# A rewritten attention phase: scores on row halves of TensorE, three bank pairs, and steps moved between engines

## The chip, the cores and the metric

The kernel runs on one core of a Trainium2 chip. The metric is the device time of one execution in microseconds (us). Engines: PE (TensorE, matmuls), PEld (its weight loads), DVE (VectorE), ACT (ScalarE), POOL (GpSimd), SP (SyncE, which here only issues DMAs). Lines L1 to L1629 are those of the kernel before.

## The reference, cut to what matters

Eight batches of 512 tokens with 256 channels go through one transformer layer in float32: a pre-norm causal attention with 16 heads of 16 channels and rotary positions, and then a mixture of 8 experts, 2 for each token.

```python
q = (x @ Wq.T + bq).reshape(b, t, h, dh).transpose(0, 2, 1, 3)      # k, v likewise; x is layer-normed
q = _apply_rope(q, cos, sin); k = _apply_rope(k, cos, sin)
scores = jnp.einsum('bhqd,bhkd->bhqk', q, k) / jnp.sqrt(dh)
scores = jnp.where(causal, scores, -jnp.inf)
out = jnp.einsum('bhqk,bhkd->bhqd', jax.nn.softmax(scores, -1), v)
x = x + out @ Wo.T + bo
logits = layernorm(x) @ router_w + router_b                         # top 2 of 8 experts, capacity 153
o = silu((e @ w_c_fc + b_c_fc) * (e @ w_gate + b_gate)) @ w_c_proj + b_c_proj
x = x + sum_k prob_k * o[expert_k, position_k]
```

## The kernel before

The program has two phases. The attention phase (`attention_phase`, L104) handles the 8 batches, the expert phase (`expert_phase`, L1081) the 8 experts; the second is the same in both kernels apart from a few semaphore counts.

**Groups and slots.** The 16 heads of a batch are 4 groups of 4 heads (g = 0 to 3). Each group takes 8 slots (u = 0 to 7), so a batch is 32 slots, and every engine has a `body_slot(b, g, u)` that issues its share in slot order. Batches 2 to 6 run in a hardware loop on each engine, the others are written out.

**Two passes over the scores.** In slot u, `pass1` (L392) makes the scores of query block i = u // 2 against all keys up to it, for the two heads of pair u % 2, and DVE takes their row maximum (`reduce_max`, L794). The maxima of a group are turned (piece M), negated on ACT (L584), and sent by DMA as one more row of the query stack (`send_max`, L333). Two groups later `pass2` (L412) makes the scores again, transposed (key block j = u // 2), now with the maximum subtracted inside the product, and ACT takes the exponential (L569, L577) into `probs`. `pv` (L437) multiplies them with V in 32-column tiles of the array, one for each of the 4 heads; being plain float32, each of its matmuls appears as two in the trace.

**The stacks.** q and k are split into a large and a small part so that three products give float32 accuracy. They go to DRAM (`store_hilo`, L315) and come back stacked (`load_stack`, L320): 64 rows, (large, small) of q against (large, large) and (small, small) of k, a row of ones and the row of the maximum. A score matmul so contracts over 65 or 66 rows of the 128. Ahead of it a bf16 matmul of a mask with the identity writes the causal mask into the bank.

**Banks.** Pass 1 uses PSUM banks 0 to 3 as two pairs, pass 2 bank 4 or 5 for one head (or two heads of 256 columns), the V product bank 6, everything else bank 7.

**Pieces.** Everything else that PE does for a batch is a piece with a slot of its own in `PIECES` (L235): X turns the normalised input of the next batch, Q is one of its four q and k projections, V its value projection, M and A turn maxima and attention output, T and O are the output projection of the batch before, H, L, R, F the router of the one before that. The rotary step is a shuffle, a multiplication by sin and a sum on DVE (L811 to L817) and a multiplication by cos on POOL (L935); the split is on POOL (L947, L950). The layer norm statistics and both normalisations (L695) are on DVE, the reciprocal square root on POOL (L898). POOL also scatters the tokens to their expert slots (L964). Some steps of the last batches are placed into the first expert by `LATE_SLOTS` (L1069).

**What sets the order.** Each engine runs its own list in program order; a wait on a semaphore holds back all that is behind it on that engine. A DMA issued by SP waits for its own condition and holds back the DMAs behind it.

## Time and profile before

| | us |
|---|---|
| median of 3 runs | 1383.12 (1378.21 to 1386.19) |
| the profiled execution | 1391.76, of it 1389.9 from the first to the last instruction |
| attention, from the first maximum to the last | 40.7 to about 593 |
| expert phase in its steady part and tail | about 691 to 1389.9 |

| engine | busy us | share |
|---|---|---|
| PE | 1238.5 | 89% |
| PEld | 1023.6 | 74% |
| DVE | 729.6 | 52% |
| POOL | 697.0 | 50% |
| ACT | 496.3 | 36% |

The granted TensorE clock is 0.943 of full speed on average. A busy PE in this profile holds the drain of each matmul too, so 89% is not 89% of what the array could do. The shares are averages over two phases with different limits, so the stages are read one by one.

### The profile page before, as it was taken

How to read it: one execution, taken by the hardware profiler on the slowest of the kernel's cores; microseconds unless marked ns; L12 is line 12 of the kernel's file. 1: busy time of each engine (PE TensorE's matmuls, PEld its weight loads, DVE VectorE, ACT ScalarE, POOL GpSimd, SP SyncE). 2: the span in 40 equal slices, each digit the busy share in tenths (PEclk: the TensorE clock that was granted, in tenths of full speed). 3: DMA queues.
4: the chain of work that ended last, by engine and by line, in shares of the span. 5: the costliest groups of instructions: out<-in, count | busy, mean ns of one | idle time of the engine just before them, and what ended most of it. 6: DMA issues, size and time to landing. Idle time of an engine off the chain costs nothing.

```text
span 1389.9 us, 25801 instructions
## 1 busy us (share of the span) xinstructions
PE 1238.5 (89%) x8360; PEld 1023.6 (74%) x8360; DVE 729.6 (52%) x1512; ACT 496.3 (36%) x988; POOL 697.0 (50%) x984
## 2 busy tenths in 40 slices
PE   3699999999898989988899999999999999997830
PEld 3465656566565656548899999999999999997730
DVE  5777776858676767556333343343333433333336
ACT  2145444535353535454223332333233332332100
POOL 4334243343425251267755665576656764634445
PEclk9699999999999999999999999999999999998865
DMA  5766545444434453432312211131122112102247
GB/s 138 216 208 193 177 115 144 109 132 103 138 93 139 100 149 93 137 124 60 96 62 91 70 62 62 64 98 54 66 78 87 54 58 70 64 28 72 69 131 249
DMA packets 82333, 147.86 MB, mean 106 GB/s; under 512 B 9263, under 2 KB 59832, under 8 KB 78142
## 3 DMA queue, kind: packets, MB, share of 16 engines
q1 hardware_dynamic: 64576, 111.37, 28.1%
q0 software_dynamic: 7936, 26.60, 5.6%
q10 hardware_dynamic: 9728, 8.67, 2.0%
q8 instruction: 56, 0.92, 0.3%
q14 instruction: 37, 0.30, 0.1%
HBM read 93.05 MB, written 53.61 MB: 106 GB/s over the span
## 4 chain that ended last, share of the span: by engine, by line
PE 45%; another core or an unknown queue 2%; DVE 1%; POOL 1%; issue 1%; DMA 0%; DVEq 0%; ACT 0%; POOLq 0%; ACTq 0%
PE ps L77 44%; PE ps L1264 1%; DVE raw L1427 1%; POOL wg_hi L1544 1%; POOL wf_hi L1544 0%; DMA wg_hi<-slot_outputs,slot_all 0%; DVE al L1417 0%; DVEq L1454 0%; DVE ah L1408 0%; POOLq L1572 0%; ACT hid L1349 0%; ACT fc L1360 0%; DVE xl L1332 0%; DVE gated L1455 0%
## 5 line engine op out<-in xcount | busy, mean ns | idle before, releaser
L1491 POOL TENSOR_TENSOR al<-hid,ah 128x384 fp32r<-128x384 f32 (+1 forms) x176 | 187.4, 1065 | 232.9 <-DVE ah L1408 232.9
L1360 ACT ACTIVATE fc<-ps,b_fc 128x384 f32<-128x384 f32 (+1 forms) x192 | 115.5, 602 | 482.4 <-PE ps L77 441.2
L1455 DVE SCALAR_TENSOR_TENSOR gated<-ps,b_gate,fc 128x384 f32<-128x384 f32 (+1 forms) x192 | 123.4, 643 | 268.1 <-PE ps L77 220.2
L794 DVE TENSOR_REDUCE mx<-ps 128x2 f32<-128x256 f32 (+3 forms) x256 | 206.6, 818 | 67.1 <-PE ps L408 56.5
L577 ACT ACTIVATE probs<-ps 128x512 f32<-128x512 f32 (+1 forms) x256 | 125.6, 541 | 73.8 <-PE ps L434 72.0
L408 PE MATMUL ps<-kst,qst 65*128 65x256 f32 (+2 forms) x512 | 151.7, 380 | 0.0
L1442 DVE TENSOR_TENSOR o_sb<-ps,b_proj 128x256 f32<-128x256 f32 x80 | 33.9, 424 | 179.0 <-PE ps L77 175.1
L569 ACT ACTIVATE probs<-ps 128x256 f32<-128x256 f32 (+1 forms) x128 | 62.6, 490 | 164.4 <-PE ps L425 150.0
L445 PE MATMUL ps<-probs,v_sb 128*32 128x512 f32 (+3 forms) x1024 | 98.8, 459 | 14.2 <-DVE v_sb L822 14.0
L77 PE MATMUL ps<-xh,wg_hi 128*128 128x384 f32 (+1 forms) x384 | 104.4, 353 | 5.0 <-DVE gated L1455 4.2
L935 POOL TENSOR_TENSOR rope_c<-qk_b,rope_table 128x512 f32<-128x512 f32 x32 | 42.7, 1333 | 128.9 <-ACT qk_b L605 128.7
L77 PE MATMUL ps<-wp_hi,ah 128*128 128x256 f32 (+1 forms) x640 | 89.7, 283 | 17.0 <-DVE al L1417 17.0
L434 PE MATMUL ps<-qst,kst 66*128 66x512 f32 (+1 forms) x256 | 103.9, 457 | 0.0
L77 PE MATMUL ps<-xh,wg_lo 128*128 128x384 f32 (+1 forms) x384 | 103.8, 352 | 0.0
L77 PE MATMUL ps<-xl,wg_hi 128*128 128x384 f32 (+1 forms) x384 | 103.8, 352 | 0.0
L1349 ACT ACTIVATE hid<-gated 128x384 f32<-128x384 f32 (+1 forms) x192 | 102.8, 535 | 1.4 <-DVE gated L1455 0.8
L77 PE MATMUL ps<-xh,wf 128*128 128x384 f32 (+1 forms) x384 | 90.6, 358 | 7.4 <-DVE xl L1332 7.3
L77 PEld LDWEIGHTS ps<-wp_hi,ah 128*128 128x128 f32 (+1 forms) x640 | 83.3, 186 | 17.9 <-issue 17.6
L77 PE MATMUL ps<-wp_hi,al 128*128 128x256 f32 (+1 forms) x640 | 88.9, 281 | 0.0
L77 PE MATMUL ps<-wp_lo,ah 128*128 128x256 f32 (+1 forms) x640 | 88.6, 281 | 0.0
L1408 DVE CAST ah<-hid 128x384 fp32r<-128x384 f32 (+1 forms) x192 | 87.7, 457 | 0.8 <-ACT hid L1349 0.8
L408 PEld LDWEIGHTS ps<-kst,qst 65*128 65x128 f32 x512 | 83.1, 204 | 2.5 <-issue 0.3
(181 smaller groups left out, 2577.5 us busy)
## 6 DMA issues: line engine op xcount, KB each, us to landing
...
qst<-qk_parts SPq DMA_DIRECT2D x64, 256.0 KB, 4.8
kst<-qk_parts SPq DMA_DIRECT2D x64, 256.0 KB, 5.2
...
```

The source lines that it names most:

```text
L77: last = nc.tensor.matmul(out, w, x, start=(i == 0), stop=(i == len(terms) - 1))
L408: last = mm(bank, qst[0:MROW, g, h, bass.ts(i, P)], kst[0:MROW, g, h, 0:width], start=False, stop=True, skip_group_check=True)
L434: mm(ps[:, S2 + hh, 0:T - q0], kst[0:ROWS, g, h, bass.ts(j, P)], qst[0:ROWS, g, h, q0:T], start=False, stop=True, skip_group_check=True).t ...
L445: last = mm(pvb[32 * h:32 * h + 32, P * j:T], v_sb[:, j, GH * g + h, :], probs[:, j % 2, h, P * j:T], start=(j == 0), stop=(j == TT - 1))
L569: A(probs[:, j % 2, 2 * pr:2 * pr + 2, P * j:T], ps[:, S2 + pr, :].rearrange("p (h q) -> p h q", h=2)[:, :, P * j - q0:T - q0], ACT.Exp, s ...
L577: A(probs[:, j % 2, 2 * pr + hh, P * j:T], ps[:, S2 + hh, P * j - q0:T - q0], ACT.Exp, scale=float(DH) ** -0.5).then_inc(exp_done, 1)
L794: V.reduce_max(mx[:, g % 2, i, 2 * pr:2 * pr + 2], both[:, :, 0:P * (i + 1)], AXX)\
L1349: A(hid[:, hc % 2, 0:width], gated[:, hc % 2, 0:width], ACT.Silu).then_inc(hid_done, 1)
L1360: A(fc[:, hc % 2, 0:width], ps[:, FC + hc % 2, 0:width], ACT.Identity, bias=b_fc[:, e, hc:hc + 1]).then_inc(fc_out, 1)
L1408: V.tensor_copy(ah[:, (8 * n + hc) % RING, 0:width], hid[:, hc % 2, 0:width]).then_inc(ah_done, 1)
L1455: V.scalar_tensor_tensor(gated[:, hc % 2, 0:width], ps[:, GATE + hc % 2, 0:width], b_gate[:, e, hc:hc + 1], fc[:, hc % 2, 0:width], ALU.ad ...
L1491: G.tensor_tensor(al[:, at, 0:width], hid[:, hc % 2, 0:width], ah[:, at, 0:width].bitcast(F32), ALU.subtract).then_inc(al_done, 1)
```

## The change

Only the attention phase is rewritten.

- **Row halves.** The stacks drop the (small, small) product: 48 rows, (large, small, large) of q against (large, large, small) of k, plus one row for the maximum. Two heads lie in one stack, one in partitions 0 to 48 and one in 64 to 112, so that each score matmul uses 64 rows of the array. The mask is made in the same way, by a matmul over 64 rows for each head (`pick_bf`).
- **Three bank pairs.** Both passes take the pairs (0, 1), (2, 3), (4, 5) in turn (`USES`), one bank for each head; bank 6 holds the pieces M, A and the V product, bank 7 the others.
- **V product.** All four key blocks are made in one pair of two-head exponentials each, at steps 5, 7, 9, 9 of a group (`PV_AT`); `probs` holds a whole group.
- **Moved steps.** Both normalisations go from DVE to ACT as scale and bias, for which POOL's reciprocal square root gets two more steps. The sin multiplication goes from DVE to POOL, the copy of V into `v_sb` from DVE to POOL, the large part of the split from POOL to ACT, the eviction of V from DVE to ACT; V's bias is folded into bo.
- **Loads.** A stack load is 8 DMAs instead of 4 (768 KB instead of 1 MB), the maximum 2 instead of 1.
- **Order.** All steps have new slots, in tables; a number of 32 or more lies in the next batch. All batches are written out, without the loop.

```diff
-MROW = ZROW + 1
+HALF = P // 2
+MROW = (NP - 1) * DH
 ROWS = MROW + 1
+PAIRS = GH // 2
 SLOTS = 8
 FILLS = 12
...
-        qst = sb("qst", [ROWS, NG, GH, T], F32R)
-        kst = sb("kst", [ROWS, NG, GH, T], F32R)
+        qst = sb("qst", [P, NG, PAIRS, T], F32R)
+        kst = sb("kst", [P, NG, PAIRS, T], F32R)
...
+        PV_AT = (5, 7, 9, 9)
+        PV_OUT_AT = 9
+        ATTN_T_AT = 10
+        ATTN_OUT_AT = 11
+        MAX_T_AT = 4
+        MAX_OUT_AT = 4
+        SEND_MAX_AT = 1
+        X_OUT_AT = (2, 4)
+        X_LOW_AT = (3, 5)
+        Q_OUT_AT = (7, 10, 11, 16)
+        COS_SIN_AT = (7, 12, 16, 21)
+        ROTATE_AT = (9, 12, 22, 25)
+        LARGE_AT = (10, 22, 23, 26)
+        SMALL_AT = (15, 20, 20, 36)
+        STORE_QK_AT = (7, 21, 26, 31)
+        LOAD_STACK_AT = (0, 3, 13, 24)
+        V_OUT_AT = (28, 31)
+        V_MOVE_AT = (18,)
+        T_OUT_AT = (22, 23)
+        X1_AT = (25, 27)
+        LOAD_XR_AT = (-7,)
+        BIAS_XR_AT = (2,)
+        STORE_X1_AT = (35,)
+        STATS1_AT = (5,)
+        RSQRT1_AT = (16,)
+        NORM1_AT = (29,)
+        LOAD_X_AT = (-5,)
+        STATS2_AT = (29,)
+        RSQRT2_AT = (34,)
+        NORM2_AT = (36,)
+        H_OUT_AT = (5, 8)
+        L_OUT_AT = (13,)
+        ROUTE_AT = (14, 16, 17)
+        PLACE_AT = (20, 24)
+        WEIGH_AT = (26,)
+        PROB_OUT_AT = (28,)
+        SCATTER_AT = (24, 25, 27, 29)
+        USES = (0, 1, 2, 0, 1, 2, 0, 1, 2, 0, 1, 2, 0, 1, 2, 0, 1, 2, 0, 1, 2, 0, 1, 2, 0, 1, 2, 1, 0, 1, 2, 0,
+                1, 2, 0, 1, 2, 0, 1, 2, 0, 1, 2, 0, 1, 2, 0, 1, 2, 0, 1, 2, 0, 1, 2, 0, 1, 2, 0, 1, 2, 0, 1, 2)
+        TILES2 = 8
...
-                sp.dma_start(qst[MROW:MROW + 1, (g - 1) % 4].bitcast(F32), negmax[:, (g - 1) % 2, :].bitcast(F32))\
-                    .then_inc(ld_max, 16)
+                for hh in range(2):
+
+                    q = rt["qk"][b, 0, :, group, :].rearrange("c (d p h) t -> h c d p t", p=PAIRS, h=2)[hh]
+                    k = rt["qk"][b, 1, :, group, :].rearrange("c (d p h) t -> h c d p t", p=PAIRS, h=2)[hh]
+                    row = HALF * hh
+                    sp.dma_start(qst[row:row + 2 * DH, g].bitcast(F32), q).then_inc(ld_stack[g], 16)
+                    sp.dma_start(qst[row + 2 * DH:row + 3 * DH, g].bitcast(F32), q[0]).then_inc(ld_stack[g], 16)
+                    sp.dma_start(kst[row:row + 2 * DH, g].bitcast(F32), k[0:1].to_broadcast([2, DH, PAIRS, T]))\
+                        .then_inc(ld_stack[g], 16)
+                    sp.dma_start(kst[row + 2 * DH:row + 3 * DH, g].bitcast(F32), k[1]).then_inc(ld_stack[g], 16)
...
+            def send_max(t):
+                wait(sp, negmax_out, t + 1)
+                wait(sp, p2_done, TILES2 * (t - 3))
+                for hh in range(2):
+                    row = HALF * hh + MROW
+                    sp.dma_start(qst[row:row + 1, t % 4].bitcast(F32), negmax[hh:GH:2, t % 2, :].bitcast(F32))\
+                        .then_inc(ld_max, 16)
...
+            def first(b, g, u):
                 i, pr = u // 2, u % 2
                 if u == 0:
-                    wait(pe, ld_stack[g], 64 * (b + 1))
-                wait(pe, red_done, 8 * s + u - 1)
+                    wait(pe, ld_stack[g], 128 * (b + 1))
+                free = pair_freed(b, g, u, 0)
+                if free:
+                    wait(pe, *free)
+                pair = pair_of(g, u, 0)
+                for hh, half in enumerate(rows_of):
+                    mm(pair[:, hh, bass.ts(i, P)], pick_bf[half, 0], causal_bf[half],
+                       start=True, stop=False, skip_group_check=True)
                 width = max(2 * P, P * (i + 1))
-                banks = scores1(u, width)
-                if i < 2:
-                    mm(ps[:, S1 + 2 * (u % 2), :].rearrange("p (h k) -> p h k", h=2)[:, :, bass.ts(i, P)], ident_bf[:],
-                       causal_bf[:].unsqueeze(1).to_broadcast([P, 2, P]), start=True, stop=False, skip_group_check=True)
-                else:
-                    for bank in banks:
-                        mm(bank[:, bass.ts(i, P)], ident_bf[:], causal_bf[:], start=True, stop=False, skip_group_check=True)
-                for hh, bank in enumerate(banks):
-                    h = 2 * pr + hh
-                    last = mm(bank, qst[0:MROW, g, h, bass.ts(i, P)], kst[0:MROW, g, h, 0:width],
+                for hh in range(2):
+                    rows = slice(HALF * hh, HALF * hh + MROW)
+                    last = mm(pair[:, hh, 0:width], qst[rows, g, pr, bass.ts(i, P)], kst[rows, g, pr, 0:width],
                               start=False, stop=True, skip_group_check=True)
                 last.then_inc(p1_done, 1)
...
+            def second(b, g, u):
+                t, g2 = 4 * b + g - 2, (g - 2) % 4
                 j, pr = u // 2, u % 2
                 if u == 0:
-                    wait(pe, ld_max, 16 * (t + 1))
+                    wait(pe, ld_max, 32 * (t + 1))
+                wait(pe, *pair_freed(b, g, u, 1))
+                pair = pair_of(g, u, 1)
                 q0 = min(P * j, T - 2 * P)
-                if u >= PAIRED:
...
-                    wait(pe, exp_done, tiles2(t, u, 0) - 2)
-                    bank = ps[:, S2 + pr, :].rearrange("p (h q) -> p h q", h=2)
...
-                    last.then_inc(p2_done, 1)
-                    return
...
+            def normalise(dst, src, rs, done):
+                for k in range(TT):
+                    ins = A(dst[:, k, :], src[:, k, :], ACT.Identity, bias=rs[:, 2, k:k + 1], scale=rs[:, 1, k:k + 1])
+                ins.then_inc(done, 1)
+
+            def normalise_input(b):
+                wait(act, rs1_done, b + 1)
+                wait(act, xT_done, 2 * b)
+                normalise(xn, x_in, rs1, xn_done)
...
+            def rotate(b, n):
+                wait(dve, cs_done, 4 * b + 4 + n + 1)
+                chain(V.stream_shuffle(qk_b[:, n % 2, :], rope_s[:, n % 2, :], SWAP))
+                V.tensor_tensor(rope_c[:, n % 2, :], rope_c[:, n % 2, :], qk_b[:, n % 2, :], ALU.add).then_inc(rope_done, 1)
...
+            def cos_sin(b, n):
+                wait(pool, qk_out, 4 * b + 4 + n + 1)
+                wait(pool, rope_done, 4 * b + 4 + n - 1)
+                wait(pool, hilo_done, 4 * b + 4 + n - 1)
+                ins = G.tensor_tensor(rope_c[:, n % 2, :], qk_b[:, n % 2, :], cos, ALU.mult)
+                if b != -1:
+                    ins = G.tensor_tensor(rope_s[:, n % 2, :], qk_b[:, n % 2, :], sin, ALU.mult)
+                ins.then_inc(cs_done, 1)
+
+            def small_part(b, n):
+                wait(pool, hilo_half, 4 * b + 4 + n + 1)
+                wait(pool, hilo_done, 4 * b + 4 + n)
+                G.tensor_tensor(hilo[:, n, 1, :], rope_c[:, n % 2, :], hilo[:, n, 0, :].bitcast(F32), ALU.subtract)\
+                    .then_inc(hilo_done, 1)
 
```

On PE, slot 1 of group 1 (pass 1 with 256 columns, then pass 2 with 512; `L77` and `L80` are the projections). Before:

```order
L401 MATMUL ps<-causal_bf,ident_bf 128x2x128 [waits red_done]
L408 MATMUL ps<-kst,qst 128x256 x2
L432 MATMUL ps<-later_bf,ident_bf 128x128 [waits exp_done]
L434 MATMUL ps<-qst,kst 128x512
L432 MATMUL ps<-later_bf,ident_bf 128x128 [waits exp_done]
L434 MATMUL ps<-qst,kst 128x512
L445 MATMUL ps<-probs,v_sb 32x128 [waits exp_done]
L445 MATMUL ps<-probs,v_sb 32x128 x3
```

Now:

```order
L437 MATMUL ps<-causal_bf,pick_bf 128x128 [waits exp_done]
L437 MATMUL ps<-causal_bf,pick_bf 128x128
L442 MATMUL ps<-kst,qst 128x256 x2
L483 MATMUL ps<-probs,v_sb 32x256 [waits exp_done]
L483 MATMUL ps<-probs,v_sb 32x256 x3
L483 MATMUL ps<-probs,v_sb 32x128 [waits exp_done]
L483 MATMUL ps<-probs,v_sb 32x128 x3
L455 MATMUL ps<-later_bf,pick_bf 128x128 [waits red_done]
L455 MATMUL ps<-later_bf,pick_bf 128x128
L459 MATMUL ps<-qst,kst 128x512 x2
L80 MATMUL ps<-xnT_hi,wk_hi 128x512 [waits xl_out,hT_out]
```

One mask matmul for both heads has become one for each; the two heads of a pass are two matmuls behind each other with nothing between them, and pass 2 has one wait where it had two. The V product (L445, now L483) stands between the two passes, twice in this slot.

On SP, the end of a batch and the load of the next stacks. Before (L331 is the stack load, L337 the maximum, L318 a store of split q or k, L359 the store of x1):

```order
L331 DMA qst<-qk_parts 32x1x2048 [waits p2_done]
L331 DMA kst<-qk_parts 32x1x2048
L331 DMA qst<-qk_parts 32x1x2048
L331 ISA
L331 DMA kst<-qk_parts 32x1x2048
L57 REGISTER_ALU
L337 DMA qst<-negmax 1x4x512 [waits p2_done,negmax_out]
L57 REGISTER_ALU
```

Now (L359 to L363 the stack load, L348 the store, L343 the input, L370 the maximum):

```order
L348 DMA qk_parts<-hilo 128x2x512 [waits hilo_done]
L343 DMA x_in<-in_x 128x4x256 [waits xn_done]
L348 DMA qk_parts<-hilo 128x2x512 [waits hilo_done]
L359 DMA qst<-qk_parts 32x2x512 [waits p2_done,st_hilo0]
L360 DMA qst<-qk_parts 16x2x512
L361 DMA kst<-qk_parts 32x2x512
L363 DMA kst<-qk_parts 16x2x512
L359 DMA qst<-qk_parts 32x2x512
L360 DMA qst<-qk_parts 16x2x512
L361 DMA kst<-qk_parts 32x2x512
L363 DMA kst<-qk_parts 16x2x512
L370 DMA qst<-negmax 1x2x512 [waits p2_done,negmax_out]
```

The last store of the split (the second L348), whose data POOL makes in slot 36, that is slot 4 of the next batch, now stands directly ahead of the 8 loads for group 1 of the next batch.

## Rows read from the trace of the kernel before

**Rows 1.** Windows view by stage: length, each engine's busy time, clock, DMA.

```profile
core 0: us, PE busy (x) PEld busy (x) DVE busy (x) ACT busy (x) POOL busy (x), PEclk, DMA share, GB/s
40.70:96.70 56.00, 50.45 (x298) 33.28 (x297) 41.29 (x67) 17.69 (x34) 19.76 (x32) 0.80 0.69 213
96.70:164.30 67.60, 65.40 (x474) 41.97 (x474) 48.73 (x87) 33.04 (x66) 25.20 (x47) 0.97 0.63 187
164.30:533.90 369.60, 342.06 (x2492) 222.00 (x2491) 263.03 (x566) 168.36 (x343) 145.23 (x245) 0.95 0.46 121
```

**Rows 2.** The windows view, the four groups of batch 3.

```profile
238.00:252.10 14.10, 13.61 (x119) 8.38 (x118) 11.18 (x27) 7.88 (x17) 2.78 (x14) 1.00 0.29 58
252.10:268.90 16.80, 16.69 (x122) 10.46 (x123) 13.26 (x33) 8.55 (x19) 5.71 (x5) 1.00 0.46 116
268.90:294.30 25.40, 20.03 (x133) 14.00 (x131) 17.17 (x33) 8.46 (x17) 17.58 (x16) 0.88 0.53 147
294.30:312.20 17.90, 17.90 (x128) 11.71 (x126) 11.11 (x26) 8.21 (x18) 2.95 (x15) 0.98 0.48 135
```

**Rows 3.** Timeline of PE, group 1 of batch 3: start, duration, what.

```profile
255.66 0.28 PE L401 MATMUL ps<-causal_bf,ident_bf 128*128 128x256 bf16 x1
...
256.02 0.23 PE L432 MATMUL ps<-later_bf,ident_bf 128*128 128x128 bf16 x1
...
256.62 0.28 PE L401 MATMUL ps<-causal_bf,ident_bf 128*128 128x256 bf16 x1
...
257.87 1.07 PE L445 MATMUL ps<-probs,v_sb 128*32 128x512 f32 x8
258.87 0.66 PE L451 MATMUL ps<-consts_sb,pv_sb 128*128 128x128 f32 x4
...
261.84 0.29 PE L405 MATMUL ps<-causal_bf,ident_bf 128*128 128x128 bf16 x2
...
262.37 0.29 PE L422 MATMUL ps<-later_bf,ident_bf 128*128 128x256 bf16 x1
...
262.82 0.85 PE L445 MATMUL ps<-probs,v_sb 128*32 128x384 f32 x8
263.61 0.20 PE L513 MATMUL ps<-onehot_bf,tri_bf 128*128 128x64 bf16 x1
```

**Rows 4.** Timeline of the weight loads (PEld) at two places.

```profile
302.86 0.16 PEld L445 LDWEIGHTS ps<-probs,v_sb 128*32 128x32 f32 x8 [0.18 <-issue]
...
304.41 0.30 PEld L408 LDWEIGHTS ps<-kst,qst 65*128 65x128 f32 x2
```

**Rows 5.** Waits view of PE, batch 3: total us, times, longest.

```profile
PE ps L445 <- DVE v_sb L822: 2.5, 1, 2.5
```

**Rows 6.** Groups view of DVE, four batches: busy us, mean ns | idle before.

```profile
L794 DVE TENSOR_REDUCE mx<-ps 128x2 f32<-128x512 f32 (+3 forms) x128 | 103.6, 817 | 28.2 <-PE ps L408 20.4 <-remote 6.0 <-issue 1.2
L812 DVE TENSOR_TENSOR rope_s<-rope_s,rope_table 128x512 f32<-128x512 f32 x16 | 15.1, 946 | 0.6
...
L697 DVE TENSOR_SCALAR hn<-x,mv,rs 128x256 f32<-128x256 f32 x16 | 5.5, 408 | 3.0 <-POOL rs L916 3.0
```

**Rows 7.** Groups view of ACT, the same four batches.

```profile
L605 ACT ACTIVATE qk_b<-ps,bqk 128x512 f32<-128x512 f32 x16 | 11.0, 687 | 14.2 <-PE ps L77 14.2
```

**Rows 8.** Groups view of POOL, the same four batches.

```profile
L964 POOL DMA_INDIRECT slot_tokens<-hn,put_at x32 | 32.2, 1006 | 15.6 <-issue 7.9 <-DVE put_at L747 7.7
L950 POOL TENSOR_TENSOR hilo<-rope_s,hilo 128x512 fp32r<-128x512 f32 x16 | 20.5, 1280 | 1.3
...
L954 POOL TENSOR_TENSOR xr<-xr,bo_all 128x1024 f32<-128x1024 f32 x4 | 11.3, 2828 | 0.0
```

**Rows 9.** Source view of line 331: ns min/median/max, first and last start.

```profile
L331 SPq DMA_DIRECT2D qst<-qk_parts x64: 562/592/1317, 31.3 to 558.2; - x64
```

**Rows 10.** The page's DMA issues: count, KB each, us from issue to landing.

```profile
kst<-qk_parts SPq DMA_DIRECT2D x64, 256.0 KB, 5.2
```

**Rows 11.** Timeline, the first score matmul of the program.

```profile
39.82 0.37 PE L401 MATMUL ps<-causal_bf,ident_bf 128*128 128x256 bf16 x1 [11.98 <-DMA kst<-qk_parts]
```

873 lines of the change are left out of this document (426 added, 447 removed), and 7 rows, old and new, of the table PIECES.

## The prediction

> **What bounds the kernel now.** I read the windows view by stage first, since the expert phase has the same work on both sides and only the stretch from 40.7 us to about 593 us can move [rows 1]. Five middle batches take 369.6 us, 73.9 us each. Per batch PE is busy for 342.06/5 = 68.4 us, DVE for 52.6, ACT for 33.7, POOL for 29.0. So PE bounds the batch, with DVE next, 21 us behind on average.
>
> Averages hide the groups, so I read batch 3 group by group [rows 2]. Groups 0, 1 and 3 take 14.1, 16.8 and 17.9 us with PE never idle for more than 0.5 us: full. Group 2 takes 25.4 us, of which PE is idle for 5.4, and the granted clock is 0.88 there. One wait of 2.5 us in it is the V product waiting for DVE's copy into `v_sb` [rows 5]. At full clock its PE work is 20.03 × 0.88 = 17.6 us. PE's work is so 14.1 + 16.8 + 17.6 + 17.9 = 66.4 us a batch, and 7.5 us of the 73.9 are stalls and clock. In group 2 DVE is busy for 17.17 us, its heaviest group: that is the next floor.
>
> **Score matmuls.** The timeline of PE, from start to start since the durations overlap, gives what one slot's pass costs now [rows 3]. Pass 1 with 256 columns takes 256.02 − 255.66 = 0.36 us, with 384 columns 262.37 − 261.84 = 0.53. Pass 2 takes 262.82 − 262.37 = 0.45 with 256 columns and 256.62 − 256.02 = 0.60 with 384. For 512 columns I continue the steps: 0.69 and 0.75. A group has two slots of each width (pass 1: 256, 256, 384, 512; pass 2: 512, 384, 256, 256): 2 × 1.94 + 2 × 2.25 = 8.4 us, or 33.5 us a batch. If the two heads, on the two row halves, stream beside each other, each pass takes half: −4.2 us a group, −16.8 a batch. No row shows two row halves at once. The nearest is the V product, four column tiles at once: from 384 to 512 columns it grows from 263.61 − 262.82 = 0.79 to 258.87 − 257.87 = 1.00 us, 0.21 for 128 columns of four heads. I take the full half; the bounds are zero and 16.8.
>
> **Tile switches.** 512 columns by that slope are 0.84 of the 1.00 us, so 0.16 us is what going into the tiled layout and out of it costs [rows 3]. Now only the V product goes in and out, 16 times a batch; after, every piece, every M and A and every V product stands among half-array passes, 37 times, 21 more. That is 21 × 0.16 = 3.4 us if the 0.16 covers both changes, and 42 × 0.15 = 6.3 if it covers one. I take 6.3, as the intercept may hide part of the drain behind the weight loads. PE's work becomes 66.4 − 16.8 + 6.3 = 56 us a batch.
>
> The Trainium skill's page "TensorEngine Tiling (Array Packing)", section Key Properties, says that changing the tiling mode drains TensorE; the 0.16 us beside the V product agrees. Its page "TensorE: Matmul & The Clock Gate", Part 3, measures 3.07 times for four row tiles, not 4; at the same share of loss (3.07/4) two halves would give an estimated 1.5 times, and the 16.8 would be about 12.
>
> **DVE.** It loses four sin multiplications of 0.946 us (3.8), eight normalisations of 0.408 (3.3) [rows 6], the eviction of V, twice a 128x512 tile, taken as ACT's tile of that size, 0.69 [rows 7] (1.4), and a copy I put at 0.4 to 1. Left are 52.6 − 8.5 − 0.7 ≈ 43.5 us; the maxima alone are 103.6/4 = 25.9 of it [rows 6], 6.5 a group. They don't shrink. The tables gather the rest unevenly: slots 24 to 31 hold the placing, x1, the statistics, a rotation and the probabilities, between 11 and 17.2 us by the groups of now [rows 2]; I take 16.5, near the heaviest, since nearly all long steps are there. PE has only about 14 there. So the batch is no longer one engine's: group by group the later of the two is about 13, 16, 13 and 16.5, together 58.5.
>
> **ACT and POOL.** A normalisation tile (128x256 with pointers) on ACT lies between 0.408, what DVE takes for it [rows 6], and 0.687, what ACT takes for twice the columns [rows 7]. I take 0.55 each: eight add 4.4 us, V 1.4, the large part at most 2.8, and the fewer exponential instructions give back some 2: ACT goes from 33.7 to about 40, under PE and DVE. The Trainium skill's page "ScalarE: Activation LUTs", section on what happens when an `exp` ACTIVATE runs, states 186 ns + 0.833 ns a column and 93 ns for each pointer operand, thus 0.585 us; eight of these would be 4.7 instead of 4.4. POOL trades the large part (4 × 1.28, [rows 8]) for sin, V's copy and rsqrt steps and ends near 34. All of this is hidden, as long as it is in time.
>
> **Waits.** An engine with 56 us of work and partners with 44, 40 and 34, in order, with three bank pairs between them, will wait now and then. The present batch has 5.4 us of idle in one group. The copy of V moves to POOL in slot 18, so the 2.5 us wait should go; the one place that I see instead is the SP queue. The last store of the split waits for POOL's slot 36. Ahead of it on POOL are eight scatters of 1.006 us with 7.9/4 = 2 us of gaps, 10 us; the bias sum, 2.83; and the split, 1.28 [rows 8]. Behind it on SP are 8 loads, 0.59 us each to issue, 4.7 us [rows 9], and 5.2 us until the last has landed [rows 10]. Slot 36 is 7 us into a group of about 13, so the loads would land at 7 + 4.7 + 5.2 = 17 us against 13 when group 1 starts; loads already under way land before that, so I count 0 to 4 and take part of it in 3.5 us of waits a batch. That makes 58.5 + 3.5 = 62 us, **−12 us a batch**.
>
> **The ends.** Batches 2 to 6: 5 × 12 = −60. Batch 1, 67.6 us long with PE busy for 65.4 [rows 1], −9, as its loads and the clock of the start press it. Batch 0, 56.0 us at a clock of 0.80 [rows 1], has only pass 1 in half its groups and many loads: −3. Batch 7 −8 with half its pieces missing, and its tail −2. The first score matmul starts at 39.82 us after waiting 11.98 for the load of kst [rows 11]: four more DMAs at 0.59 are +2.4 [rows 9] and the normalisation on ACT, 4 × 0.15 more, behind other work of ACT, +1; then slot 1 turns batch 1's input, which the same chain makes late by another 4 to 5. Together +8. The last batch's chain at the expert phase has two more rsqrt steps and ACT's slower normalisation: +1. Sum: −60 − 9 − 3 − 8 − 2 + 8 + 1 = **−73 us**. From the profiled execution, 1391.8, that is 1319; the median of the runs is 8.7 us lower, so **1310 us**.
>
> **The rivals.** *Smooth* (0.20): the switches hide behind the weight loads (the 8 loads of a V product fit in 0.16 us, [rows 4]) and DVE's uneven slots are bridged by three bank pairs. The period is PE's 56 or less, −18 a batch and so on in the ends: −115, 1268. For it speaks that DVE's average is only 43.5.
>
> *Weight loads in series* (0.15): two full loads take 0.30 us [rows 4], more than half of a pass of 256 columns. If the pair's loads don't hide, a pass costs no less than 0.33 to 0.4 us and a group 5.7 instead of 4.2; PE is at 61 to 62, the period 68: −32 in all, 1351. Against it: now the loads hide behind the matmul ahead.
>
> *The late queue* (part of the forecast's range): if the 4 us before group 1 are lost in every batch, the period is 66 and the time 1330.
>
> *Halves one after another, the other side* (0.12): no row shows two row halves running together, and the score passes stay at 33.5 us. The 6.3 us of switches and the 1.5 us of second mask matmuls come on top: PE 66.4 + 7.8 = 74, with the same waits 78 to 80, +5 a batch and +8 at the start: +42, 1425. It decides the sign from where the pairing saves less than about 8 of the 16.8 us. That each of the two products is now 48 rows deep instead of 65 saves nothing by itself, since by [rows 3] the time of a pass goes by its columns and nothing there goes by rows; no row shows otherwise.
>
> The Trainium skill's page "TensorEngine Tiling (Array Packing)", section PSUM Bottleneck, warns that tiling speeds up TensorE, not what empties the banks. As a mechanism of this kernel that is the forecast itself: the maxima stay at 25.9 us a batch and DVE sets groups 1 and 3.
>
> **How the numbers follow.** My forecast has 0.48, smooth 0.20, loads in series 0.15, one after another 0.12, and 0.05 for about no change (two losses of the above together, about 1383). The range from 1262 to 1370 holds the first three. Half a per cent, 7 us, is about what a measurement of this kernel can tell from no change. Faster by more: 0.48 + 0.20 + 0.15 less 0.01 for their edges = 0.82; within: 0.05; slower: 0.12 + 0.01 = 0.13.
>
> **What would show it.** In the profile after: two score matmuls of a pair with starts less than 0.05 us apart and 0.2 to 0.35 us from pass to pass; the five middle batches at 62 us each; PE busy for less than 58 us in each and DVE for about 44; group 3 the longest or level with group 1, PE waiting there for the maxima; a wait on `kst` or `qst` at slot 0 of group 1 of at most 4 us; the first score matmul at 43 us. I am wrong if the pair's starts are a full matmul apart, if the period is over 68 us, or if PE waits for an engine in a group where I have it level.

## The result and the profile of the changed kernel

| | before | changed |
|---|---|---|
| median | 1384.65 us (4 runs, 1378.21 to 1395.65) | 1480.3 us (4 runs, 1475.04 to 1485.32) |
| ratio | | 1.068, 95% interval 1.060 to 1.077 |
| profiled span | 1389.9 us, clock 0.943 | 1483.3 us, clock 0.881 |

The changed kernel is slower by 6.8%; the forecast was 5% faster. In short: the score matmuls on row halves and the moved steps do nearly what the sum said, but the new stack loads run over 2 of the 16 DMA engines. With that mended, the change makes the kernel 3% faster. A part of what the batches lose is a standstill that some chips show and others don't; it is told apart below.

The head of its page, with the 40 slices of the span:

```profile
PE 1210.3 (82%) x8620; PEld 964.0 (65%) x8620; DVE 675.9 (46%) x1398; ACT 543.3 (37%) x968; POOL 727.7 (49%) x1024
...
PE   3237978888788888686789999999999999999840
...
PEclk9557797888797979787899999999999999999865
```

PE is busy for 28 us less than before, and the program is 93 us longer: PE waits, and then works at a lower clock. The windows view by stage (columns as in [rows 1]), for batch 0, batch 1 and batches 2 to 6:

```profile
47.20:142.60 95.40, 47.48 (x314) 27.23 (x316) 34.83 (x56) 22.22 (x36) 20.77 (x33) 0.64 0.33 114
142.60:216.10 73.50, 62.53 (x496) 35.03 (x496) 39.28 (x72) 36.36 (x58) 25.33 (x36) 0.85 0.44 155
216.10:603.00 386.90, 319.65 (x2645) 181.30 (x2645) 231.77 (x482) 195.87 (x325) 167.58 (x259) 0.84 0.31 100
```

From start to start of a batch's first score matmul, the batches 2 to 6 take 77.4 us each. So of the 93 us, the later start is 7.4 (47.18 against 39.82), batch 0 is 39.1 (95.4 against 56.3), batch 1 is 7.1, batches 2 to 6 are 18.1 (386.9 against 368.8, both from start to start) and all after that 21.7. The waits view of PE over the attention phase:

```profile
PE ps L437 <- DMA kst<-qk_parts: 75.8, 13, 18.0
PE ps L437 <- DVE mx L852: 32.1, 3, 29.2
PE ps L483 <- ACT negmax L607: 20.3, 6, 5.4
PE ps L465 <- ACT hn L628: 15.5, 6, 9.8
```

PE waits 75.8 us for stack loads in 13 places, of them 18.0 before the first score matmul (11.98 in the kernel before, [rows 11]) and 4.6 to 8.2 at the start of group 1 in nearly every batch. The third line, whose long waits lie in group 3, is not the loads' doing: it is there with the loads mended too (23.1 us in batches 2 to 6 of r7) and belongs to the standstill below. The 29.2 us for DVE's maxima are the loads once removed, as the waits view of DVE around batch 0 shows:

```profile
DVE stats L737 <- DMA x_in<-in_x: 34.8, 1, 34.8
```

DVE stood at the statistics of batch 2's input, with all maxima behind them, since SP had issued that load only behind 24 stack loads. In the timeline of SP each pair of halves looks like this (start, duration of the issue):

```profile
47.95 0.64 SPq L359 DMA_DIRECT2D qst<-qk_parts  x1
48.63 2.48 SPq L360 DMA_DIRECT2D qst<-qk_parts  x1
51.14 0.64 SPq L361 DMA_DIRECT2D kst<-qk_parts  x1
51.82 2.36 SPq L363 DMA_DIRECT2D kst<-qk_parts  x1
54.23 0.64 SPq L359 DMA_DIRECT2D qst<-qk_parts  x1
54.91 2.01 SPq L360 DMA_DIRECT2D qst<-qk_parts  x1
```

The issues of about 0.6 us of [rows 9] have become 2.0 to 2.5 for nearly every second one here, up to 4.1; the 24 of the start go from 39.7 to 79.5 us. The rows of L360 and L363 are the small loads of 16 rows, each held up behind the large one ahead of it. The windows view of such a stretch, first of the changed kernel, then of the kernel before:

```profile
49.00:64.00 15.00, 8.48 (x40) 4.89 (x38) 4.31 (x6) 1.88 (x3) 3.04 (x3) 0.50 0.30 112
```

```profile
42.00:53.00 11.00, 8.17 (x30) 5.43 (x30) 8.84 (x19) 1.19 (x2) 4.06 (x16) 0.50 1.02 204
```

The last two columns are the DMA share and GB/s. The same job of loading stacks has all 16 engines busy before and 0.30 of them now. Counted from the starts and lengths of the data packets of SP's queue in the trace: in these 15 us of the changed kernel, exactly 2 are in flight for 9.6 us; in the 11 us of the kernel before, exactly 16 for 8.8. The large loads of the changed kernel have the shape (part 2, d 16, head 2, 512 columns), those before (d 16, part 2, 2048 columns).

What a stall costs beyond itself is seen in batch 5, in windows of 3 us around the start of group 1:

```profile
465.00:468.00 3.00, 1.91 (x18) 0.78 (x16) 1.23 (x1) 1.46 (x3) 2.44 (x2) 1.00 0.57 205
468.00:471.00 3.00, 0.00 (x0) 0.00 (x0) 0.00 (x0) 0.00 (x0) 0.05 (x1) 0.65 0.19 67
471.00:474.00 3.00, 1.25 (x12) 0.85 (x12) 0.60 (x3) 0.00 (x0) 0.00 (x0) 0.50 0.23 75
474.00:477.00 3.00, 3.00 (x27) 1.50 (x24) 1.50 (x3) 1.91 (x3) 0.00 (x0) 0.50 0.18 65
477.00:480.00 3.00, 3.00 (x13) 1.96 (x13) 0.22 (x1) 1.29 (x2) 0.00 (x0) 0.65 0.20 67
480.00:483.00 3.00, 3.00 (x25) 1.97 (x23) 1.37 (x4) 2.11 (x5) 2.79 (x3) 1.00 0.13 49
```

PE is idle for 5.8 us, and until about 479 the granted clock is at the lower level of 1.2 GHz (0.50). The 6 us of work in that stretch would take half as long at the upper level.

The wait for the load is not all that the batches lose. The windows view of batch 4, its four groups:

```profile
374.05:395.85 21.80, 13.47 (x128) 7.43 (x126) 9.97 (x21) 11.48 (x20) 6.71 (x18) 0.87 0.29 90
395.85:414.35 18.50, 18.48 (x139) 10.27 (x139) 11.09 (x22) 8.71 (x14) 9.56 (x19) 0.78 0.19 69
414.35:427.65 13.30, 12.83 (x129) 7.26 (x128) 11.99 (x26) 9.34 (x15) 4.82 (x6) 1.00 0.30 96
427.65:452.25 24.60, 18.32 (x138) 10.88 (x139) 13.93 (x32) 9.96 (x17) 13.30 (x17) 0.79 0.46 141
```

Against the same groups with the loads mended (r13 below: 14.8, 14.9, 13.3, 15.4), the 7.2 us of waiting for kst at the end of group 0 and the lower clock in group 1 (3.6 us) are the loads' part. The 9.2 us more in group 3 are another thing, and mending the loads doesn't remove them on such a chip (r7).

### The profile page after: what moved, and what is told of

Same layout as the page of the kernel before. It is cut to its first block and busy times, and to the rows that moved or that the text cites. A ratio compares the mean times of both kernels' runs of the same rounds, so it can differ in the third digit from the quotient of the medians.

```text
span 1483.3 us, 24480 instructions
## 1 busy us (share of the span) xinstructions
PE 1210.3 (82%) x8620; PEld 964.0 (65%) x8620; DVE 675.9 (46%) x1398; ACT 543.3 (37%) x968; POOL 727.7 (49%) x1024
## 5 line engine op out<-in xcount | busy, mean ns | idle before, releaser
L601 ACT ACTIVATE probs<-ps 128x1024 f32<-128x1024 f32 (+3 forms) x256 | 177.3, 701 | 203.2 <-PE ps L459 189.7
L437 PE MATMUL ps<-causal_bf,pick_bf 64*128 64x128 bf16 x512 | 64.3, 247 | 118.1 <-DMA kst<-qk_parts 75.8
L437 PEld LDWEIGHTS ps<-causal_bf,pick_bf 64*128 64x128 bf16 x512 | 26.6, 100 | 169.1 <-DMA kst<-qk_parts 62.6
L483 PE MATMUL ps<-probs,v_sb 128*32 128x512 f32 (+3 forms) x1024 | 105.7, 514 | 20.8 <-ACT negmax L607 20.3
L442 PE MATMUL ps<-kst,qst 48*128 48x256 f32 (+2 forms) x512 | 119.0, 463 | 0.0
L459 PE MATMUL ps<-qst,kst 49*128 49x256 f32 (+2 forms) x512 | 115.5, 449 | 0.0
L80 PE MATMUL ps<-xh,wg_hi 128*128 128x384 f32 (+1 forms) x384 | 104.9, 355 | 6.8 <-DVE gated L1509 6.8
L80 PE MATMUL ps<-xh,wg_lo 128*128 128x384 f32 (+1 forms) x384 | 103.9, 352 | 0.0
L80 PE MATMUL ps<-xl,wg_hi 128*128 128x384 f32 (+1 forms) x384 | 103.7, 352 | 0.0
L80 PE MATMUL ps<-wp_hi,ah 128*128 128x256 f32 (+1 forms) x640 | 90.3, 284 | 14.3 <-DVE al L1471 14.3
L455 PEld LDWEIGHTS ps<-later_bf,pick_bf 64*128 64x128 bf16 x512 | 25.9, 97 | 107.0 <-issue 49.8
L80 PEld LDWEIGHTS ps<-wp_hi,ah 128*128 128x128 f32 (+1 forms) x640 | 83.9, 187 | 15.3 <-issue 14.9
L80 PE MATMUL ps<-xh,wf 128*128 128x384 f32 (+1 forms) x384 | 89.9, 356 | 4.6 <-ACT fc L1414 3.2
L80 PE MATMUL ps<-wp_hi,al 128*128 128x256 f32 (+1 forms) x640 | 89.6, 283 | 0.0
L80 PE MATMUL ps<-wp_lo,ah 128*128 128x256 f32 (+1 forms) x640 | 89.2, 282 | 0.0
```

The costliest lines, as they stand in the source:

```text
L80: last = nc.tensor.matmul(out, w, x, start=(i == 0), stop=(i == len(terms) - 1))
L437: mm(pair[:, hh, bass.ts(i, P)], pick_bf[half, 0], causal_bf[half], start=True, stop=False, skip_group_check=True)
L442: last = mm(pair[:, hh, 0:width], qst[rows, g, pr, bass.ts(i, P)], kst[rows, g, pr, 0:width], start=False, stop=True, skip_group_check=True)
L459: last = mm(pair[:, hh, 0:T - q0], kst[rows, g2, pr, bass.ts(j, P)], qst[rows, g2, pr, q0:T], start=False, stop=True, skip_group_check=True)
L483: last = mm(low[32 * h:32 * h + 32, P * j:T], v_sb[:, j, GH * group + h, :], probs[:, t % 2, h, PROB_AT[j]:PROB_AT[j + 1]], start=(j == 0) ...
L601: A(probs[:, t % 2, 2 * pr:2 * pr + 2, PROB_AT[j]:PROB_AT[j + 1]], pair_of(g, u, 1)[:, :, P * j - q0:T - q0], ACT.Exp, scale=float(DH) ** ...
```

## The experiments

The sixteen runs are spread over four chips, r1 to r4, r5 to r8, r9 to r12 and r13 to r16. Chips differ: the kernel before took 1340 us on the first, 1391 on the second, 1341 on the third and 1334 on the fourth. So each run is told as a ratio to the kernel before on its own chip, or set against the other runs on that chip. The expectations in us of r1 to r3 were written against the 1384.65 us above.

| run | edit | median us | ratio (95%) |
|---|---|---|---|
| r1 | changed kernel, loads over 16 engines | 1296.0 | 0.968 (0.965 to 0.972) |
| r2 | changed, large loads cut into 16-row loads | 1343.2 | 1.003 (1.000 to 1.005) |
| r3 | changed, input of batch 2 loaded early | 1442.9 | 1.079 (1.076 to 1.083) |
| r4 | before, loop written out | 1336.0 | 0.998 (0.996 to 1.000) |
| r5 | changed, again | 1484.9 | 1.064 (1.054 to 1.074) |
| r6 | r1 and normalisations on DVE | 1355.4 | 0.971 (0.960 to 0.981) |
| r7 | r1 and input of batch 2 early | 1358.3 | 0.974 (0.965 to 0.983) |
| r8 | changed, last store of the split later | 1467.8 | 1.052 (1.042 to 1.062) |
| r9 | r1 again | 1297.7 | 0.968 (0.966 to 0.970) |
| r10 | r1 and scatters apart | 1293.0 | 0.964 (0.962 to 0.966) |
| r11 | r6, r7 and r10 together | 1317.2 | 0.981 (0.978 to 0.985) |
| r12 | before, loads over 2 engines | 1612.7 | 1.204 (1.201 to 1.206) |
| r13 | r1 again | 1296.2 | 0.972 (0.966 to 0.977) |
| r14 | r6 again | 1337.1 | 1.000 (0.997 to 1.003) |
| r15 | r10 again | 1294.4 | 0.970 (0.964 to 0.975) |
| r16 | r7 and r10 together | 1292.6 | 0.968 (0.963 to 0.973) |

**The loads over 16 engines (r1).** The order (d, part, head, columns) doesn't fit into one DMA while a half's two heads lie apart. So the half takes heads 0 and 1, or 2 and 3, which are neighbours in DRAM; the V product picks its `probs` accordingly.

```diff
-q = rt["qk"][b, 0, :, group, :].rearrange("c (d p h) t -> h c d p t", p=PAIRS, h=2)[hh]
+q = rt["qk"][b, 0, :, group, :].rearrange("c (d h p) t -> h d c (p t)", p=PAIRS, h=2)[hh]
...
-    probs[:, t % 2, h, PROB_AT[j]:PROB_AT[j + 1]]
+    probs[:, t % 2, 2 * (h % PAIRS) + h // PAIRS, PROB_AT[j]:PROB_AT[j + 1]]
```

> The changed kernel with one edit: the heads of a group are laid into the pairs so that the two heads of one row half lie next to each other in DRAM, and each stack load runs over (d, part, 1024 columns) with 16 as its outermost size instead of (part, d, head, 512) with 2. Same 8 loads, same bytes. Theory A (two DMA engines): in the changed kernel the loads with an outermost size of 2 have 2 packets in flight for most of their time, where the kernel before has 16; so a stack takes 10 to 14 us to land and the start of batch 0 and group 1 of every batch wait for it. Then this run has the 24 loads of the start issued in under 20 us instead of 39.9, no wait of PE for kst over 1 us after batch 0, and a time of 1390 to 1420. Theory B (the number of DMAs and the place of the store in SP's list): nothing of that changes, 1470 to 1485.

Measured: ratio 0.968 instead of 1.068. Theory A's 1390 to 1420 us are ratios of 1.004 to 1.026, so the gain is larger than expected. The chip explains little of that: on the second, where the changed kernel takes 1484.9 us (r5), the one with mended loads takes 1358.3, 0.974 (r7, which also loads batch 2's input early). The 24 loads of the start are issued in 16.9 us, after batch 0 PE waits for kst only 1.2 us in two places, and batches 2 to 6 take 58.8 us each. SP's timeline at the start, and the windows view (batches 2 to 6, then a stretch of loads):

```profile
41.84 0.58 SPq L363 DMA_DIRECT2D kst<-qk_parts  x1
42.47 0.67 SPq L359 DMA_DIRECT2D qst<-qk_parts  x1
43.17 0.58 SPq L360 DMA_DIRECT2D qst<-qk_parts  x1
```

```profile
157.80:451.70 293.90, 280.21 (x2651) 161.86 (x2649) 229.81 (x483) 194.64 (x326) 165.00 (x255) 0.99 0.42 133
42.00:57.00 15.00, 7.99 (x38) 5.03 (x38) 4.30 (x6) 3.27 (x6) 3.08 (x14) 0.50 0.69 212
```

The edit also makes packets of 4096 bytes out of 2048, and changes which dimension comes first. The next run takes these apart.

**More loads, smaller, over 16 engines (r2).** Each large load becomes two of 16 rows, with 2048 byte packets, 12 DMAs for a stack.

```diff
-sp.dma_start(qst[row:row + 2 * DH, g].bitcast(F32), q).then_inc(ld_stack[g], 16)
+for c in range(2):
+    sp.dma_start(qst[row + c * DH:row + (c + 1) * DH, g].bitcast(F32), q[c]).then_inc(ld_stack[g], 16)
...
```

> The changed kernel with each load of 2 x 16 rows written as two loads of 16 rows: 12 DMAs for a stack instead of 8, packets of 2048 bytes as before, outermost size 16 everywhere. Theory A (two DMA engines): the loads land sooner although there are more of them; a stack costs 12 x 0.6 = 7.2 us of issue; 1400 to 1435. Theory B (the number of DMAs): half as many again make the start and group 1 later, over 1495.

Measured: 1343.2 us, 1.003, again below theory A's range (1.011 to 1.036 as a ratio). There are half as many again DMAs, the packets are as small as in the changed kernel, and the ratio is lower by 0.06. So neither packet size nor the number of DMAs was the main cause. The 47 us over r1 come with loads that are late again (a wait for kst of 28.2 us in 8 places against 11.4 in 3); whether the number of DMAs or their half-size packets cost them, no run took apart.

**The same fault put into the kernel before (r12).**

```diff
-q = rt["qk"][b, 0, :, group, :].rearrange("c (d h) t -> d c (h t)", h=GH)
+q = rt["qk"][b, 0, :, group, :].rearrange("c (d h) t -> c d (h t)", h=GH)
...
```

> The kernel before with one edit: the rows of a stack load in the order (part, d) instead of (d, part), so that the outermost size of each load is 2 instead of 16; same 4 loads, same bytes, packets of 8192 bytes. Theory A (the outermost size sets over how many of the 16 DMA engines a load is spread): 2 packets in flight instead of 16; a packet took 0.33 to 0.65 us, so a stack of 128 packets needs at least 128 x 0.33 / 2 = 21 us and four of them 84 us a batch: the period rises from 69 to 74 us to at least 84, the time by 80 us or more, over 1.06. Rival (packet size or the number of DMAs is what matters, not the order of dimensions): within 1 per cent of the kernel before.

Measured: 1612.7 us, 1.204; batch 0 takes 112 us and batches 1 to 6 take 94 to 102 each. Bytes, packets and number of DMAs are those of the kernel before. In some 24 us near its start (31 to 55), 2 packets are in flight for 18. In SP's timeline an issue is held up for up to 10 us, and PE waits for kst:

```profile
36.45 0.65 SPq L331 DMA_DIRECT2D qst<-qk_parts  x1
37.14 10.00 SPq L331 DMA_DIRECT2D kst<-qk_parts  x1
47.18 4.32 SPq L331 DMA_DIRECT2D qst<-qk_parts  x1
```

```profile
PE ps L401 <- DMA kst<-qk_parts: 141.6, 23, 27.5
```

With r1, r2 and r12 theory A is shown from both sides: mending the outermost size removes the waits, and putting size 2 into the kernel before brings them there.

**SP's order (r3, r7, r8).** r3 and r7 issue the input of batch 2 behind the load of stack 1:

```diff
-            for g in range(1, NG):
-                load_stack(0, g)
-            load_x(2)
+            load_stack(0, 1)
+            load_x(2)
+            for g in range(2, NG):
+                load_stack(0, g)
```

> The changed kernel with the load of batch 2's input issued behind the load of stack 1 instead of behind stack 3 in SP's list of the start. DVE waits 34.8 us in batch 0 for that input, with all maxima behind it. If the order of SP's list is what costs there, batch 0 loses 25 to 30 us of its 95.4 and the time is 1452 to 1462. If the loads themselves bound batch 0 (they need 40 us in either order), groups 1 to 3 wait for kst instead, and less than 12 us are gained: 1468 or more.

> The changed kernel with the head layout, and the load of batch 2's input behind the load of stack 1 in SP's list of the start. PE is idle 5.95 us in group 1 of batch 0 with DVE waiting for that input. If SP's order still costs: batch 0 goes from 62.4 to 56 to 58 us, 4 to 6 us faster than the head layout alone, ratio 0.963 to 0.965. If the load of stacks 2 and 3 then comes late, batch 0 stays within 1 us.

In r3 batch 0 takes 83.1 us instead of 95.4 (96.1 in r5): 12 to 13 us, near the second reading, as groups 2 and 3 then take 23 us each, waiting for their late stacks. Its time in us can't be set against the expectation, which was written for the slower chip, and the changed kernel itself was not run on r3's chip; the ratio of 1.079 is no better than that of the changed kernel. In r7 batch 0 takes 60.0 us against 62.4, 67.1 and 65.8 in r1, r9 and r13 on other chips: 2.4 to 7 us. On one chip, r16 against r15 below, batch 0 goes from 64.9 to 60.5 us and the time by 1.8 us, which is within the intervals.

r8 moves the last store of the split behind the load for group 1, which is the late queue of my prediction:

```diff
-        STORE_QK_AT = (7, 21, 26, 31)
+        STORE_QK_AT = (7, 21, 26, 34)
```

> The changed kernel with only the last store of the split moved behind the load for group 1 in SP's list (from slot 31 to slot 2 of the next batch); loads over 2 engines as they are. If the place in the queue (my prediction's late queue) costs the wait for kst at group 1 of each batch: that load is issued 4 to 5 us sooner, the wait of 4.6 to 8.2 us goes, and with the clock that falls behind it a batch is 6 to 9 us shorter: 30 to 50 us less than the changed kernel. If the two slow engines cost it, the load lands later than its issue anyway, shared with the load for group 2: under 15 us less.

Measured: 1467.8 against 1484.9 us for the changed kernel on the same chip (r5, at 1.064 where 6 to 8% over the kernel before were expected), 17 us less, a little over what the second reading gave. The wait for kst falls from 81.9 us in r5 to 52.1, and batches 4 to 6 take 71.7 us against 73 to 80. So the place in the queue was real but the smaller part; with the loads over 16 engines hardly any wait is left for it to cause (r1).

**The loop (r4).** The changed kernel has no loop, and its engines load 16384 bytes of instructions every 13 to 25 us, where the kernel before loads none from 235 to 543 us.

```diff
-            with pe.Fori(2, 7) as b:
+            for b in range(2, 7):
...
```

> The kernel before with batches 2 to 6 written out instead of in a hardware loop; nothing else. In its trace there is no instruction packet from 235 to 543 us, in the changed kernel one of 16384 bytes every 13 to 25 us, and once a batch ACT, DVE and PE stand still together for 4 to 5 us while the token scatters run and such a packet lands. Theory C (code loading): +8 to +25 us over the kernel before, with such a standstill in some of batches 3 to 6. Rival: the standstill is the changed kernel's own chain of waits, and this one is within 4 us of the kernel before.

Measured: 0.998 (0.996 to 1.000), and r4's trace has such packets of instructions in the batches where the kernel before has none. Theory C falls, on this chip: written out, the batches cost nothing.

**The normalisations (r6, r11, r14, r13).** One of the moved steps, undone on top of r1: DVE subtracts the mean and multiplies, in the same slots of the batches, and the reciprocal square root is two steps shorter.

```diff
-    ins = A(dst[:, k, :], src[:, k, :], ACT.Identity, bias=rs[:, 2, k:k + 1], scale=rs[:, 1, k:k + 1])
+    ins = V.tensor_scalar(dst[:, k, :], src[:, k, :], mv[:, k, 0:1], rs[:, 1, k:k + 1], ALU.subtract, ALU.mult)
...
```

> The changed kernel with the head layout that loads over 16 engines, and both normalisations back on DVE (subtract the mean, multiply), the reciprocal square root two steps shorter; slots unchanged. With them on ACT, PE waited for ACT's normalised tiles 14.5 us at the very start, 6.1 in batch 0, 1.1 in each later batch, and 10.0 and 6.1 in the first expert. Theory D (the move to ACT costs at the ends and is free in the middle): the waits at the start and in the first expert shrink by 0.5 to 1.3 us each, the period of the batches stays within 0.5 us of 58.4, since DVE with 3.3 us more is at about 47; 2 to 5 us faster than the head layout alone (ratio to the kernel before 0.963 to 0.968). Rival (DVE's slots 24 to 31 are nearly full, so the move to ACT is what makes the period): the period grows by 1 to 3 us, +6 to +18 us, ratio 0.972 to 0.982.

> The head layout with both normalisations on DVE, scatters where the changed kernel has them. In the run with all edits DVE was busy for 16.5 of the 18.1 us of group 3, PE waited for maxima, and the granted clock fell to 0.66 in the next group 0. Theory F (it is DVE's load in group 3 that the move to ACT takes away): on a chip where the base has group 3 at 15.3 us, group 3 takes 17 to 18.5 us here and the batch 62 to 66 us instead of 58.4: +20 to +35 us over the base. On a chip where the base has the standstill in group 3, the standstill hides it: within 6 us of the base. Rival (the scatters moved apart made DVE wait there, not the normalisations): the batch stays at 58 to 59 us and this run is 2 to 5 us faster than the base.

r6 told nothing: on its chip group 3 takes 23 to 25 us either way (below), 0.971 against 0.974 of r7. r14 against r13, on one chip, tells it: 1337.1 against 1296.2 us. The move to ACT is worth 41 us, more than theory F had, and the whole gain of the mended kernel over the one before: r14 keeps the row halves and all else, and its ratio is 1.000. The windows view of one batch, its four groups, first with them on ACT (r13):

```profile
277.50:292.30 14.80, 13.56 (x130) 7.49 (x126) 10.25 (x21) 10.87 (x19) 5.91 (x20) 1.00 0.50 151
292.30:307.20 14.90, 14.90 (x140) 8.38 (x139) 10.59 (x22) 9.19 (x15) 10.35 (x19) 1.00 0.31 101
307.20:320.50 13.30, 12.83 (x129) 7.27 (x128) 11.99 (x26) 9.34 (x15) 5.30 (x9) 1.00 0.30 98
320.50:335.90 15.40, 14.44 (x137) 9.13 (x136) 13.48 (x32) 9.85 (x17) 12.02 (x11) 1.00 0.60 188
```

and with them on DVE (r14), with the waits view of PE for the same batch:

```profile
294.90:315.30 20.40, 20.24 (x128) 10.65 (x126) 11.90 (x25) 9.46 (x15) 3.40 (x8) 0.60 0.34 112
315.30:330.20 14.90, 14.90 (x140) 8.39 (x139) 10.59 (x22) 9.20 (x15) 10.36 (x19) 1.00 0.27 90
330.20:343.50 13.30, 12.83 (x129) 7.27 (x128) 11.99 (x26) 9.34 (x15) 4.89 (x7) 1.00 0.31 97
343.50:361.60 18.10, 14.50 (x137) 9.13 (x136) 16.49 (x36) 8.13 (x13) 13.98 (x20) 1.00 0.55 164
```

```profile
PE ps L455 <- DVE mx L844: 4.0, 4, 2.6
```

Groups 1 and 2 are equal to 0.1 us. In group 3 DVE goes from 13.48 to 16.49 us of work and the group from 15.4 to 18.1. PE waits at its end for maxima, 2.6 us at once. The group 3 before the rows shown ends in the same wait, from 291.8 to 294.5 us, and group 0 behind it runs at a clock of 0.60 instead of 1.00: 20.4 instead of 14.8 us. Three us of DVE's work cost 8.3 us in this batch (7.4 on average of batches 2 to 6), two thirds of them by the clock in a group where DVE isn't even late.

**All edits (r11), and the scatters apart (r10, r15, r16).** The eight token scatters go out two each at slots 24, 27, 30 and 33.

```diff
-        SCATTER_AT = (24, 25, 27, 29)
+        SCATTER_AT = (24, 27, 30, 33)
...
```

> The head layout that loads over 16 engines, once more, as the base for the other runs of this call on the same chip. On one chip its group 3 took 15.3 us in every batch, with the early load of x on another 23 to 24 us, with a standstill of PE, ACT and DVE of 4 to 5 us while the token scatters run and the slow clock behind it. Ratio to the kernel before 0.965 to 0.978 on either.

> The head layout, with the eight token scatters of a batch issued two each at slots 24, 27, 30 and 33 instead of 24, 25, 27 and 29. Theory E (the standstill in group 3 is the eight scatters in a row, during which signals between engines come late): on a chip where the base shows it, the standstill is cut in parts of under 1.5 us, group 3 takes 16 to 19 us instead of 23 to 24, 30 to 45 us less in all. Rival (it is the traffic of loads and stores of group 3, whatever the scatters do): group 3 stays within 1.5 us. On a chip where the base has group 3 at 15.3 us: no difference over 3 us.

> The head layout, the scatters apart, the normalisations back on DVE and the load of batch 2's input early, together. By the single runs: 2 to 3 us each from the normalisations at the start and in group 0 of the batches and from the early load, and the gain of the scatters apart where there is one: 3 to 8 us below the run with the scatters apart alone.

> The head layout that loads over 16 engines, as the base of this call. Ratio to the kernel before 0.966 to 0.978.

> The head layout with the token scatters apart. On the chip without the standstill it was at 0.9641 against 0.9681 of the base, which may be noise. Theory E (eight scatters in a row make the standstill): on a chip where the base of this call shows group 3 at 23 us, group 3 is 16 to 19 us and the run 30 to 45 us faster than the base. Rival: group 3 stays within 1.5 us of the base. Without the standstill: within 5 us of the base.

> The head layout, the scatters apart and the load of batch 2's input early, with the normalisations on ACT as in the changed kernel. The early load took batch 0 from 67 to 60 us: 3 to 7 us faster than the scatters apart alone, the fastest of the kernels here.

r9 and r13 repeat r1. The scatters apart are 4.6 and 1.8 us below their base (expected was at most 3 and 5), within what the intervals leave. r11 missed its expectation by 27 us or more, and pointed to r14: it has the normalisations on DVE. r16 is the fastest kernel on the fourth chip, 1292.6 against 1296.2 us of r13, also within the intervals; against r15 it is 1.8 us faster, where 3 to 7 were expected. r10 and r16 are 3.6% and 3.2% faster than the kernel before.

**A standstill that some chips show.** In the first trace of the changed kernel, and in r5 to r8, all on the second chip, ACT, DVE and PE stand still together for 3 to 6 us in group 3 while the scatters run. The waits view of ACT in batches 3 to 5 of r7, and of batches 2 to 5 in r13, its longest line:

```profile
ACT v_next L624 <- remote: 11.9, 3, 4.9
```

```profile
ACT probs L601 <- PE ps L459: 50.9, 57, 2.2
```

"remote" means that no event in the profile explains the end of the wait; r13 has none, nor have the runs on the first and third chip. On the second chip group 3 takes 23 to 25 us instead of 15.4, the mended kernel's batches 67.3 us (r7) instead of 58.6, and the kernel before is 50 us slower too. The trace of the kernel before that the prediction was read from has it as well, in group 2, where its own scatters are: `<-remote 6.0` for DVE in [rows 6], and a group 2 of 25.4 us where r4 takes 21 to 22. So in both kernels it lies where the scatters are. In one of these standstills of r7 (278.1 to 281.6 us) the nearest packets of instructions are at 271.6 and 292.9, so it isn't code loading alone. The run that should tell (r15) fell on a chip without it. Its cause stays open.

## Why the prediction was wrong, step by step

**What bounds it: right.** PE was the bound of the kernel before, and DVE's heaviest group the next floor: r14 shows it. But the group 2 of 25.4 us that I read is 3 to 4 us longer than in r4, with the standstill in it, and my 7.5 us of stalls and clock took that for the kernel's own: written out on a chip without the standstill (r4), the kernel before has a period of 69.0 us, not 73.9.

**Score matmuls: right but for the narrow passes.** I took half of a pass, 0.18 us for 256 columns and 0.35 to 0.375 for 512. The timeline of PE in the changed kernel:

```profile
335.61 0.63 PE L80 MATMUL ps<-xnT_hi,wk_lo 128*128 128x512 f32 x2
336.07 0.63 PE L80 MATMUL ps<-xnT_lo,wk_hi 128*128 128x512 f32 x2
336.63 0.23 PE L437 MATMUL ps<-causal_bf,pick_bf 64*128 64x128 bf16 x2
...
336.87 0.23 PE L455 MATMUL ps<-later_bf,pick_bf 64*128 64x128 bf16 x2
...
337.23 0.23 PE L437 MATMUL ps<-causal_bf,pick_bf 64*128 64x128 bf16 x2
```

Pass 1 with 256 columns takes 336.87 − 336.63 = 0.24 us for both heads, against 0.36 in [rows 3]; pass 2 with 512 takes 337.23 − 336.87 = 0.36, against 163.69 − 162.98 = 0.71 in the timeline of the kernel before, shown below, where I had continued to 0.75. With 384 columns it is 0.30 (r13). A group's passes are then 4.6 us, not 4.2, and the saving about 15 us a batch of my 16.8. The halves do run together. The rival of halves one after another, to which I gave the slower outcome, falls, and so does that of the weight loads in series (0.33 to 0.4 us a pass): the slower outcome came from elsewhere.

```profile
162.98 0.23 PE L432 MATMUL ps<-later_bf,ident_bf 128*128 128x128 bf16 x1
...
163.69 0.60 PE L465 MATMUL ps<-consts_sb,mx 128*4 128x128 f32 x4
```

**Tile switches: of the right size.** The projection ahead starts 336.63 − 336.07 = 0.56 us before the first half-array matmul, and 0.46 before another projection (335.61 to 336.07 us): 0.09 to 0.10 us for one change. 42 of them are about 4 us a batch, nearer to my 3.4 than to the 6.3 that I took. With the loads mended PE is busy for 280.21/5 = 56.0 us a batch; I had 56. That this fits so well is partly luck: the switches were too dear by as much as the passes were too cheap. The Trainium skill's page "TensorEngine Tiling (Array Packing)", section Key Properties, says that changing the tiling mode drains TensorE. The trace agrees, with 0.09 us.

**DVE, ACT, POOL: right to 3 us.** 46.0, 38.9 and 33.0 us a batch in r1, against my 43.5, 40 and 34. A normalisation tile took 0.586 us on ACT against my 0.55. I called that move hidden, and named no price for its absence: it is 41 us. The estimate of 0.585 us, worked out from the figures of the Trainium skill's page "ScalarE: Activation LUTs" (they stand in its section "What ACT_TABLE_LOAD costs"), agrees with the 0.586.

**The groups: right in sum, without the standstill.** 14.8, 14.9, 13.3 and 15.4 in r13, 58.4 together, against my 13, 16, 13 and 16.5, 58.5 together; single groups were off by up to 1.8 us, and the 3.5 us of further waits didn't come. On the second chip it is 67.3 us a batch (r7), so my 62 lies between two chips.

**Waits: this step failed.** I priced the 8 loads by count, 0.59 us to issue and 5.2 us to land, from rows of loads that were spread over 16 engines [rows 9, 10]. "I count 0 to 4 and take part of it in 3.5 us of waits a batch" was a sum over a queue whose speed I took as given. With its first dimension of 2, each large load has 32 packets of 0.084 us on each of 2 engines, 2.7 us, and a stack has four of them: about 11 us instead of 5. The diff in the text ahead of the prediction shows it: `h c d p t` puts c, the part, ahead of d, where L326 of the kernel before has `d c (h t)`. That put the wait at group 1 at 5 to 8 us instead of 0 to 4, with 3 to 4 us more by the clock behind it: some 10 us a batch (77.2 us in r5 against 67.3 in r7, on one chip). The other 9 us, from the 58.6 of r13 to the 67.3 of r7, go with the standstill, which my sum put at nothing although [rows 6] had it as `remote`.

**The ends: this step failed too.** I had +8 for the start and −3 for batch 0; batch 0 alone was +39.1, from the same loads and the input behind them in the list. That the start itself was +7.4 is luck: with the loads mended, and the four more issues and ACT's normalisation still there, the first score matmul starts at 40.4 us (r1) against 39.5 in r4. The normalised tiles of the last batches also come late, with the loads mended: around the end of attention and in the first expert PE waits 16.1 us in 2 places for ACT's `hn` in r1, and 2.2 us for DVE's in r4. I had 1 us for it. It isn't ACT's doing, as r6 and r14 have it as well; the new slots of the last batches are the likely reason, which no run took apart.

**The sum with the loads mended.** The traces of r1 and r4 come from one chip, and r4 is the kernel before in all but the loop. Start and batch 0 together are +5.5 us (I had +5), batch 1 −10.1 (−9), batches 2 to 6 −51.4 (−60), and all from the start of batch 7 on +13.8, where I had −9. Together −42 instead of −73. So even with good loads the sum is 31 us too low, 23 of them behind the start of batch 7.
